# Two late tiles of a masked attention kernel have a third quarter of their probabilities turned by DMA

## The reference

```python
q = x @ Wq.T + bq;  k = x @ Wk.T + bk;  v = x @ Wv.T + bv
scores = q @ k.T / sqrt(128)
scores = where(adj > 0, scores, -9e15)          # adj: 4096 x 4096 int32
att = softmax(scores, axis=-1) @ v
out = layernorm(x + elu(att), eps=1e-5)          # no scale, no shift
```

## Time and profile before

| | |
|---|---|
| median of three runs | 434.64 us |
| the profiled execution | 434.69 us, of it span 432.9 us |
| granted TensorE clock, mean | 0.996 |
| busy: TensorE, VectorE, ScalarE, GpSimd | 98%, 84%, 82%, 79% |
| period 31 of TensorE | 399.66 to 411.88 us |
| first value matmul of tile 31 | 421.29 us |
| first instruction of tile 31's end (L643) | 427.08 us |

### The profile page before, as it was taken

The page is one execution under the profiler, slowest core; times in us unless marked ns, Lnnn a source line. Parts: engine busy times, 40 slices in busy tenths (PEclk is TensorE's granted clock), DMA queues, the critical chain, the costliest instruction groups (busy, mean ns, idle before and its releaser), DMA issues.

```text
span 432.9 us, 11401 instructions
## 1 busy us (share of the span) xinstructions
PE 422.1 (98%) x3479; PEld 311.0 (72%) x3479; DVE 364.0 (84%) x671; ACT 354.9 (82%) x737; POOL 343.6 (79%) x613
## 2 busy tenths in 40 slices
PE   8999899999999999999999999999999999999994
PEld 6564577777777777777777777777777777777783
DVE  1788898888889898888889888888899988888783
ACT  4779878888888888888888988888888988888892
POOL 0065558889888988898888888898889888898874
PEclk9999999999999999999999999999999999999998
DMA  8934999999999999999999999999999999999550
GB/s 225 380 109 125 262 268 229 264 228 267 279 276 277 264 248 264 277 265 257 251 279 262 262 242 279 266 259 252 270 267 264 247 263 282 261 256 229 103 104 20
DMA packets 149932, 104.76 MB, mean 242 GB/s; under 512 B 133024, under 2 KB 141728, under 8 KB 141728
## 3 DMA queue, kind: packets, MB, share of 16 engines
q1 hardware_dynamic: 149488, 104.41, 91.5%
q10 hardware_dynamic: 432, 0.20, 0.2%
HBM read 69.47 MB, written 2.10 MB: 165 GB/s over the span
## 4 chain that ended last, share of the span: by engine, by line
POOL 58%; issue 18%; PE 17%; ACT 3%; DVE 2%; POOLq 2%; ACTq 0%; DVEq 0%
POOL p_rows L322 25%; POOL res L336 6%; POOL rstd L360 4%; POOL neg_mean L347 3%; POOL y L341 3%; POOL att_sum L329 3%; POOL var L356 3%; POOL att L331 3%; PE ps_out L819 3%; POOL centred L349 2%; POOL expm L338 2%; POOL var_eps L358 2%; PE ps_t L720 2%; PE ps_scores L780 2%; PE ps_scores L781 2%
## 5 line engine op out<-in xcount | busy, mean ns | idle before, releaser
L322 POOL TENSOR_TENSOR p_rows<-scores,p_rows 128x256 f16<-128x256 f32 x252 | 175.9, 728 | 8.3 <-ACT p_rows L470 8.3
L591 DVE CUSTOM_DVE_ANT_0 scores<-ps_scores,adj 128x1024 f32<-128x1024 f32 x128 | 156.0, 1219 | 14.5 <-issue 11.1
L453 ACT ACTIVATE scores<-scores,neg_max 128x1024 f32<-128x1024 f32 x128 | 145.7, 1138 | 2.3 <-DVE neg_max L600 2.3
L606 DVE TENSOR_TENSOR p_lo<-ps_t,p_hi 128x512 f16<-128x512 f32 x124 | 82.6, 685 | 27.9 <-ACT p_hi L462 27.5
L577 DVE TENSOR_SCALAR adj<-adj 128x1024 f32<-128x1024 int32 x128 | 104.9, 820 | 0.0
L780 PE MATMUL ps_scores<-k_hi,q_hi 128*128 128x512 f16 x256 | 97.1, 379 | 0.1
L781 PE MATMUL ps_scores<-k_lo,q_hi 128*128 128x512 f16 x256 | 97.0, 379 | 0.0
L782 PE MATMUL ps_scores<-k_hi,q_lo 128*128 128x512 f16 x256 | 97.0, 379 | 0.0
L819 PE MATMUL ps_out<-v_parts,p_hi 128*128 128x256 f16 x496 | 95.3, 273 | 0.7 <-DVE p_lo L606 0.7
L819 PE MATMUL ps_out<-v_parts,p_turned 128*128 128x256 f16 x496 | 95.0, 273 | 0.0
L821 PE MATMUL ps_out<-v_parts,p_lo 128*128 128x128 f16 x496 | 88.5, 219 | 0.0
(11 more groups left out here) (92 smaller groups left out, 474.3 us busy)
## 6 DMA issues: line engine op xcount, KB each, us to landing
adj<-in_adj_dram SPq DMA_DIRECT2D x64, 1024.0 KB, 5.3
out_dram<-y_out SPq DMA_DIRECT2D x32, 64.0 KB, 5.0
x_rows<-in_x_dram SPq DMA_DIRECT2D x4, 256.0 KB, 4.0
x_rows<-in_x_dram SPq DMA_DIRECT2D x2, 512.0 KB, 6.0
p_turned<-p_rows SPq DMA_TRANSPOSE x63, 4.5
w_rows<-in_L_gnn_Wq_dram ACTq DMA_DIRECT2D x1, 64.0 KB, 2.5
w_rows<-in_L_gnn_Wk_dram ACTq DMA_DIRECT2D x1, 64.0 KB, 3.2
w_rows<-in_L_gnn_Wv_dram ACTq DMA_DIRECT2D x1, 64.0 KB, 3.8
```

The costliest lines, as they stand in the source:

```text
L322: last = nc.gpsimd.tensor_tensor(p_rows[c][:, w:][:, cols], s_sb[s][:, c * PIECE:c * PIECE + w][:, cols], p_rows[c][:, 0:w][:, cols], ALU. ...
L453: nc.scalar.activation(s_sb[s][:, cols], s_sb[s][:, cols], ACT.Exp, bias=neg_max[:, s:s + 1], accum_out=p_sums[:, s, c:c + 1]).then_inc(ex ...
L591: nc.vector.tensor_tensor_reduce(out=s_sb[s][:, cols], in0=ps_scores[c % 2][:, :], in1=mask_sb[s][:, cols], scale=SCALE, scalar=-3.0e38, o ...
L606: nc.vector.tensor_tensor(p_lo[:, k, :], ps_t[bank_of(s, g)][:, :], p_hi[:, k, :], ALU.subtract).then_inc(plo_ready, 1)
```

## The change

Tiles 29 and 30 (`LATE`) no longer have groups 4 and 5 transposed by TensorE. ScalarE copies the two groups as one piece of 1024 columns to float16 (`extra_high`, at step 7 of period p for tile p-1), VectorE subtracts it to get the low half (`extra_low`, at the end of step 7, behind the row maximum), and SyncE issues a third DMA transpose for the tile (`turn_extra`). The rows and the turned columns lie in the first and second quarter of `x_t`; there is one such buffer, so the second tile's copy waits for the first tile's turn and its turn for the first tile's values. The counting semaphores of the removed steps are raised by `sem_inc` alone.

The values of these two tiles come in the order `LATE_ORDER` = 0, 1, 6, 2, 7, 3, 4, 5. Behind the last period the order on TensorE is now: transposes 6, values 0, 1, transposes 7, values 6, 2, 7, transposes 2 and 3 of tile 31, values 3, 4, 5, then as before. TensorE's and ScalarE's loops end one round earlier, and their last two periods are written out. On SyncE turn 1 of tile 29 and its extra turn come ahead of the store of tile 27, and the extra turn of tile 30 directly behind its turn 1, ahead of the store of tile 28 and of the turn of tile 31.

```diff
+LATE_ORDER = (0, 1, 6, 2, 7, 3, 4, 5)
+EXTRA = (4, 5)
...
+        extra_rows = x_t[:, 0:PIECE].bitcast(F16)
+        extra_cols = x_t[:, PIECE:2 * PIECE].bitcast(F16).rearrange("p (b r) -> p b r", r=P)
...
+        LATE = (TILES - 3, TILES - 2)
+        def order_of(i):
+            return LATE_ORDER if isinstance(i, int) and i in LATE else PV_ORDER
+        def has_extra(i):
+            return isinstance(i, int) and i in LATE
...
-            return STEPS * i + PV_ORDER.index(g) + 1
+            return STEPS * i + order_of(i).index(g) + 1
...
                 sp.dma_start_transpose(p_turned[c][s][:, :, :], p_rows[c][:, :]).then_inc(turned[c], 16)
+            def turn_extra(i):
+                sp.wait_ge(extra_lo, LATE.index(i) + 1)
+                if i == LATE[1]:
+                    sp.wait_ge(pv_done, pv_count(LATE[0], EXTRA[1]))
+                sp.sem_inc(turn_begun, 1)
+                sp.dma_start_transpose(extra_cols, extra_rows).then_inc(extra_turned, 16)
...
             period(TILES - 2, 0, loads=False)
-            period(TILES - 1, 1, head=False, loads=False)
+            turn(LAST - 2, 1, 1)
+            turn_extra(LAST - 2)
+            period(TILES - 1, 1, head=False, loads=False, turns_1=False)
             turn(LAST - 1, 0, 1)
+            turn_extra(LAST - 1)
             store(LAST - 3, 0)
...
+            def extra_high(i, s):
+                n = LATE.index(i)
+                act.wait_ge(exp_done, exp_count(i, EXTRA[0] // 2))
+                if n:
+                    act.wait_ge(extra_turned, 16 * n)
+                nc.scalar.activation(extra_rows[:, 0:PIECE], s_sb[s][:, EXTRA[0] * BANK:EXTRA[0] * BANK + PIECE],
+                                     ACT.Copy).then_inc(extra_hi, 1)
+                act.sem_inc(phi_ready, len(EXTRA))
             def attention(i, s):
...
                     for g in range(FIRST_PE, STEPS):
-                        if T_AT[g] + 1 == j + STEPS and has_2:
+                        if T_AT[g] + 1 == j + STEPS and has_2 and not (g in EXTRA and has_extra(p - 2)):
                             high_part(p - 2, n, g, not warm and p == 2)
-                        if T_AT[g] + 1 == j and has_1:
+                        if g == EXTRA[0] and T_AT[g] + 1 == j and has_1 and has_extra(p - 1):
+                            extra_high(p - 1, 1 - n)
+                        elif T_AT[g] + 1 == j and has_1:
                             high_part(p - 1, 1 - n, g, not warm and p == 1)
...
             period(3, 1)
-            with act.Fori(2, TILES // 2) as pair:
+            with act.Fori(2, TILES // 2 - 1) as pair:
                 for n in range(2):
                     period(2 * pair + n, n)
-            high_part(LAST - 1, 0, 5, False)
+            period(TILES - 2, 0)
+            period(TILES - 1, 1)
             exp_piece(LAST, 1, 0, False)
...
                                         ALU.subtract).then_inc(plo_ready, 1)
+            def extra_low(i, s):
+                dve.wait_ge(extra_hi, LATE.index(i) + 1)
+                nc.vector.tensor_tensor(extra_rows[:, PIECE:2 * PIECE], s_sb[s][:, EXTRA[0] * BANK:EXTRA[0] * BANK + PIECE],
+                                        extra_rows[:, 0:PIECE], ALU.subtract).then_inc(extra_lo, 1)
+                dve.sem_inc(plo_ready, len(EXTRA))
...
                     for g in range(FIRST_PE, STEPS):
-                        if T_AT[g] + 1 == j + STEPS and has_2:
+                        if T_AT[g] + 1 == j + STEPS and has_2 and not (g in EXTRA and has_extra(p - 2)):
                             low_part(p - 2, n, g)
-                        if T_AT[g] + 1 == j and has_1:
+                        if T_AT[g] + 1 == j and has_1 and not (g in EXTRA and has_extra(p - 1)):
                             low_part(p - 1, 1 - n, g)
...
                         row_max(p, n)
+                    if j == 7 and has_1 and has_extra(p - 1):
+                        extra_low(p - 1, 1 - n)
                     if j == 1 and has_2:
...
             period(TILES - 1, 1, makes_mask=False)
-            low_part(LAST - 1, 0, 5)
             reciprocal(LAST - 1, 0)
...
                 pe.wait_ge(exp_done, exp_count(i, g // 2))
-                if first and k < 2:
+                if has_extra(i):
+                    pe.wait_ge(plo_ready, PE_GROUPS * (i - 1) + k + 1)
+                elif first and k < 2:
                     pe.wait_ge(proj_lo, last_user(bank))
...
+            def extra_counts():
+                pe.sem_inc(pt_ready, len(EXTRA))
             def values(i, s, g, first):
-                if g >= FIRST_PE:
+                order = order_of(i)
+                extra = g in EXTRA and has_extra(i)
+                if extra:
+                    if g == EXTRA[0]:
+                        pe.wait_ge(extra_turned, 16 * LATE.index(i) + 16)
+                elif g >= FIRST_PE:
                     pe.wait_ge(plo_ready, PE_GROUPS * i + g - FIRST_PE + 1)
-                elif g % 2 == 0 or pv_count(0, g - 1) > pv_count(0, g):
+                elif g % 2 == 0 or order.index(g - 1) > order.index(g):
                     pe.wait_ge(turned[g // 2], 16 * i + 16)
-                if g == PV_ORDER[0] and not first:
+                if g == order[0] and not first:
                     pe.wait_ge(att_ready, i - 1)
...
                     k = g * BLOCKS + b
-                    if g >= FIRST_PE:
+                    if extra:
+                        high = extra_cols[:, (g - EXTRA[0]) * BLOCKS + b, :]
+                        low = extra_cols[:, len(EXTRA) * BLOCKS + (g - EXTRA[0]) * BLOCKS + b, :]
+                    elif g >= FIRST_PE:
                         high = p_hi[:, g - FIRST_PE, b * P:(b + 1) * P]
...
                     nc.tensor.matmul(ps_out[s][:, 0:2 * D], high, v_parts[:, k, :],
-                                     start=(g == PV_ORDER[0] and b == 0), stop=False)
+                                     start=(g == order[0] and b == 0), stop=False)
                     last = nc.tensor.matmul(ps_out[s][:, D:2 * D], low, v_parts[:, k, D:2 * D],
-                                            start=False, stop=(g == PV_ORDER[-1] and b == BLOCKS - 1))
+                                            start=False, stop=(g == order[-1] and b == BLOCKS - 1))
                 last.then_inc(pv_done, 1)
...
                             transposes(p - 2, n, g, False)
-                        if T_AT[g] == j and has_1:
+                        if g == EXTRA[0] and T_AT[g] == j and has_1 and has_extra(p - 1):
+                            extra_counts()
+                        elif T_AT[g] == j and has_1 and not (g in EXTRA and has_extra(p - 1)):
                             transposes(p - 1, 1 - n, g, not warm)
                     if has_2:
-                        values(p - 2, n, PV_ORDER[j], first)
+                        values(p - 2, n, order_of(p - 2)[j], first)
...
             period(3, 1)
-            with pe.Fori(2, TILES // 2) as pair:
+            with pe.Fori(2, TILES // 2 - 1) as pair:
                 for n in range(2):
                     period(2 * pair + n, n)
+            period(TILES - 2, 0)
+            period(TILES - 1, 1)
             transposes(LAST - 1, 0, 6, False)
-            values(LAST - 1, 0, 4, False)
             values(LAST - 1, 0, 0, False)
...
             transposes(LAST - 1, 0, 7, False)
-            values(LAST - 1, 0, 5, False)
-            values(LAST - 1, 0, 6, False)
+            for g in (6, 2, 7):
+                values(LAST - 1, 0, g, False)
             last_transposes(2)
             last_transposes(3)
-            for g in (7, 2, 3):
+            for g in (3, 4, 5):
                 values(LAST - 1, 0, g, False)
```

More of the change, by code:

```diff
@@ L142, in attention_kernel @@
         turn_begun = sem("turn_begun")
+        extra_hi = sem("extra_hi")
+        extra_lo = sem("extra_lo")
+        extra_turned = sem("extra_turned")
         rows_hi = sem("rows_hi")
```

## The result

The changed kernel takes 439.6 us (median of 4 runs, 438.12 to 440.24) against 434.65: ratio 1.0109, 95% interval 1.0083 to 1.0135. It is slower, as forecast, but by 5.0 us and not by 1.5, and outside the range (435.1 to 437.5). The profiled execution took 439.84 us, its span is 438.0. Up to 396 us it runs as before.

A forecast was written before the change was run, and what follows sets the result against it. TensorE was taken to bound the kernel to 411.88 us, then the arrivals from VectorE and DMA; + 1.77 (last transposes later) - 0.25 (an absorbed wait) = + 1.52 on 434.69, 436.2 us, range 435.1 to 437.5.

The forecast's parts named there:

- Part 4 (b): Behind the last period: values 2 of tile 30 wait for turn 1, landing 4.6 us after issue; last transposes 1.77 us later.
- Rival A: TensorE alone counts: every removed transpose shortens the kernel, 1.75 us in all and no new wait, 432.9 us; chance 0.06.
- Part 1, ScalarE and TensorE: Period 30, tile 29: exp starts at 398.90, its transposes at 400.18; TensorE stands 0.75 us, keeping 0.13 of 0.88.
- Part 1, VectorE's wide subtraction: Period 30: one 1024-column subtraction replaces two low parts, taken as 1.14 us, ending near 401.4, at no cost.
- All that follows on ScalarE and GpSimd moves by 0.13 and no more: From period 30's copy of group 6 on, both engines run 0.13 us earlier; turn 1 of tile 30 is issued at 412.44.
- the two gaps behind the last period: TensorE idle about 1.4 us ahead of values 6 (VectorE's low part) and about 1 us ahead of values 2 (DMA).
- Part 2: Period 31: values 2 of tile 29, moved from step 6 to step 3, wait 0.36 us for their turn, issued at 400.95.
- Part 3: End of period 31: tile 30's last exp holds TensorE's transposes of group 6 until 411.84, against 411.88 before.
- Part 4 (c): Behind the last period: tile 30's extra turn lands at 419.55, values 4 want it at 419.99, so just free.
- Rival C: Turn 1 or the extra turn lands late; a landing after 5.9 us gives + 2.82, 437.5 us; chance 0.18.

The follow-up runs named there:

- e1: The changed kernel's new value order and written-out loops, but no extra turn (groups 4 and 5 stay with TensorE): 438.04 us, 1.0072 to the kernel before.
- e6: The changed kernel with another order behind the last period (values 7 directly after 6, values 2 after transposes 2 and 3 of tile 31): 438.37 us.
- e2: The changed kernel with ScalarE's last exp piece ahead of the 1024-wide copy in the two periods: 439.03 us.
- e5: The kernel before with only TensorE's and ScalarE's loops ended one round earlier and the last two periods written out: 434.93 us, 1.0003.
- e8: The changed kernel with the extra turn for tile 30 alone and e6's order behind the last period: 435.88 us, 1.0024 to the kernel before.
- e4: The changed kernel with 12 identity transposes ahead of values 6 and 12 ahead of values 2 of tile 30, filling TensorE's gaps: 438.13 us.
- e11: e6 with 8 identity transposes ahead of values 6 and 4 ahead of values 7 of tile 30, filling the gaps: 436.94 us.
- e3: The changed kernel with VectorE's wide subtraction one place later, behind the mask of step 7: 439.21 us, 1.0117 to the kernel before.

## Why the prediction was wrong, step by step

- **Direction and skeleton: right.** Part 4 (b) held: values 2 of tile 30 stand ahead of a landing. e1 shows the loss without the extra turn, e6 shows the wait of values 2 go (0.19 us) with another order. Rival A had nothing: 1.75 us of transposes shed, and no kernel's median below that of the kernel before.
- **Part 1, ScalarE and TensorE: right** (exp 398.91, transposes 400.19). e2 takes the stall away and gains nothing clear of the spread.
- **Part 1, VectorE's wide subtraction, "That costs nothing here": a step that failed.** Its own time was right (1.21 us, ending 401.4). What I priced was VectorE's queue alone. It took 1.0 us from GpSimd, the engine that the turns hang on, so turn 1 of tile 30 was issued at 413.31 instead of 412.44: + 0.87. "All that follows on ScalarE and GpSimd moves by 0.13 and no more" fell with it. The experiments bear it out: from the turn near 395 us to this one it is 17.50 to 17.56 us in the four kernels without the operation in period 30 (before, e1, e5, e8), and 17.93 to 18.28 in the nine with it.
- **Part 4 (b), the landing: mis-sized.** 5.6 us for 4.6; behind the issue at 413.31 TensorE goes on at 418.94, 5.63 later where I had 4.70, so + 0.93. Why it lands later is open (e5). I had the 5.1 of the same turn in the earlier trace rows and chose the median of sixteen.
- **Not in the sum at all: the clock, the largest step that failed.** I forecast the two gaps behind the last period (1.4 and 1.0 us; they were 1.57 and 1.41) and priced them as waiting time only, which puts the clock at nothing without a reason. The 1.67 us of slow matmuls is the largest of the three terms. e4 and e11 show that it goes when the gaps are filled.
- **The sum closes.** 0.87 + 0.93 + 1.67 = 3.47. The forecast had tile 31's values at 421.31 + 1.75 = 423.06; they start at 426.54, 3.48 later. This holds for the profiled execution. Without the clock's term the account is 436.2 + 0.87 + 0.93 = 438.0 us, near the run of 438.12 with its higher mean clock and still outside the range; so the forecast fails without the fall as well.
- Part 2: right in kind, the stall 1.39 for 0.36, again mostly by GpSimd's microsecond (turn 1 issued at 402.02 for 400.95). Part 3: right mechanism, 412.71 for 411.84. Part 4 (c): the extra turn of tile 30 was free (values 4 wait for nothing). Rival C had the lateness, at 0.18; it lacked the clock.

The Trainium skill, page "GPSIMD Engine Reference", section "1. Specifications", lists GpSimd's SBUF interfaces as shared with VectorE, with contention when VectorE's instruction has two SBUF inputs. The traces agree and give the size (1.67 us for 0.67). The Trainium skill, page "Runtime: NRT & Kernel Launch", section "Instruction fetch mechanics", calls the cost of crossing a block mostly hidden. For the time of the kernel that is so (e5, 1.0003); the turn in flight landed later in the same run (6.2 us for 4.6).

## What to carry to other kernels

Price a moved operation on the engine that it shuts out as well as on its own: in this kernel a VectorE operation of 1.2 us with both inputs in SBUF held GpSimd by up to 1.0 us and made turn 1 of tile 30, which hangs on GpSimd, 0.4 to 0.7 us late, in both places that were tried. When a new order puts a late arrival ahead of ready work, the price is the wait and, in about half of the runs here with such gaps, the slow clock behind it; put the ready work first. Matmuls shed in the middle of this kernel were worth nothing, since its end hangs on a transfer that does not move.

## What the hardware showed that I had not expected

- VectorE and GpSimd shut each other out, and the one that started first kept its length: the wide subtraction took 1.21 us when it came first by 0.07 us, and GpSimd's 0.67 us became 1.67; it took 1.57 and 1.69 when it came second (e6, e3).
- A mask operation of 1024 columns (one SBUF input, 0.68 us) did the same to GpSimd in e3 (1.14 us for 0.67). It does so in the kernel before as well: beside the mask of 403.93 us GpSimd's subtraction at 404.14 takes 1.12 us.
- The clock fell behind gaps of 1.57 and 1.41 us in the changed kernel's profiled run. It did not fall behind 1.84 and 1.59 us in e2's or behind 0.89 and 1.52 us in e1's, and one of e6's four runs stayed up. The length of the gaps alone does not decide it; what does is open.
